# A decoder kernel: in the last cross attention, the scores of both row tiles of a head pair are issued back to back

## The chip, the cores and the metric

The kernel runs on one core of one Trainium2 chip. The metric is the device time of one execution in microseconds (us). Before the change three executions took 4450.89, 4462.71 and 4469.61 us (median 4462.71). For so small an edit the spread matters: the three lie 0.4% apart.

## The reference, cut to what matters

The kernel computes two decoder layers of self attention, cross attention and experts, each behind a layer norm, for 16 sequences of 256 rows and 256 channels. The change touches only the cross attention of the second layer. It has 16 heads of 64 channels; the keys of a sequence are 256 from one source and 256 from a second, 512 in all, and only the first 256 are masked:

```python
k_new = jnp.concatenate([k, gk], axis=1)            # 512 keys per sequence
q = (queries @ Wq.T + bq).reshape(b_s, nq, H, D_K).transpose(0, 2, 1, 3)
att = jnp.einsum('bhqd,bhdk->bhqk', q, k_new) * scale
att_k = jnp.where(attention_mask, -jnp.inf, att[..., :nk])
att = jnp.concatenate([att_k, att[..., nk:]], axis=-1)
att = jax.nn.softmax(att, axis=-1)
out = jnp.einsum('bhqk,bhkd->bhqd', att, v_new)
out = out.transpose(0, 2, 1, 3).reshape(b_s, nq, H * D_V)
return out @ Wo.T + bo
```

## The kernel before, in words

Keys and values of this attention are made in an earlier stage and read back by DMA. The stage itself is `wide_attention_phase`, which writes out one program for each engine. For each sequence `b` it runs 16 steps `s`. A step is one pair of heads (group `g = s // 2`) and one row tile of 128 rows (`t = s % 2`), so that an even step and the odd one behind it share their heads and keys. In this text the even step and the odd step behind it are called a pair of steps, and (8, 9) is the pair of steps 8 and 9.

Each item `n` (one step's work) goes through the engines like this:

- TensorE forms its scores (`scores`, L784): six matmuls of 512 columns into one of two score buffers `s_ps[s % 2]`. A head has 64 channels, so the two heads use the two halves of the array's rows at the same time: three products of two matmuls. It first waits until the buffer has been read (`m_ready`).
- VectorE adds the mask and takes the row maximum (`row_max`, L624), which also frees the score buffer.
- ScalarE takes the exponentials and their sums (`exps`, L714).
- VectorE takes the reciprocals (L685), GpSimd multiplies by them (L581, `n_ready`).
- TensorE transposes the result (`turn`, L796, eight transposes of 128 columns), and VectorE (L630) and ScalarE (L722) copy one half each out of PSUM.
- In a later step TensorE multiplies by the values (L851), ScalarE (L737) and VectorE (L663) take the result.

In step `s` TensorE issues the scores of `s + 2`, the transposes of `s - 1`, and then what the table `AT_STEP` names for the step in one of two banks `a_ps`. At odd steps that is a product with the values (O0 to O7). At even steps it is, in turn: nothing (0), the output projection (2 and 4, L805), the transposes of the normalised rows (6, L835), and the queries of the next sequence (8, 10, 12, 14, L841, Q0 to Q3). The banks are handed back by `a_free`: Q1 for instance waits until VectorE has taken Q0's other half (L647).

The order of each engine is the order in which it is written, with semaphores between them. On ScalarE a step is: exponentials of `s + 1`, copy of transposed `s - 1`, rounding of what the step's bank holds, and at even steps rounding of a key group (L745). On VectorE: reciprocal of `s`, maximum of `s + 2`, copy of `s - 1`, then the work on the banks; `add_output` (L679) in step 4. On GpSimd: multiplication of `s`, and at odd steps the rest of a key group (L575). The sequences 1 to 14 run in a hardware loop of two sequences per turn; the others are written out.

Of the kernel before, what the change touches and what calls it, by code (L numbers as in the profile page):

```python
# [34 lines left out]
TT = S // P  # L35
# [339 lines left out]
def wide_attention_phase(nc, c, x_res, ident, ins, kv):  # L375
# [4 lines left out]
    PAIRS, NS = H // 2, H  # L380
# [3 lines left out]
    with ExitStack() as ctx:  # L384
# [83 lines left out]
        def of(use):  # L468
            return -1 if use in (O7, OUT) else 1 if use == Z or use in QUERIES else 0
# [4 lines left out]
        def emptied(b, use):  # L474
            return (b + 1) * 7 + use // 2 + 2

        def exists(b):
            return not isinstance(b, int) or 0 <= b < B
# [18 lines left out]
        def later(b, s, steps):  # L497

            return b + (s + steps) // NS, (s + steps) % NS

        with nc.Block() as block:
# [263 lines left out]

            @block.tensor
            def _(pe):
                def scores(b, s, u):
                    if not exists(b):
                        return  # L770
                    g, t = s // TT, s % TT
                    n = b * NS + s
                    out = s_ps[s % 2]
                    if t == 0:
                        pe.wait_ge(k_split, b * PAIRS + g + 1)
                    if s % 4 == 0:
                        q = (Q0, Q1, Q2, Q3)[g // 2]
                        pe.wait_ge(a_free[q % 2], emptied(b - 1, q))
                    if not (isinstance(n, int) and n < 2):
                        pe.wait_ge(m_ready, n - 1)  # L780
                    for q_piece, k_piece in PIECES:
                        for i in range(2):
                            lane = slice(i * c.dk, (i + 1) * c.dk)
                            e = pe.matmul(out[:, i, :], qT[q_piece][lane, g, t * P:(t + 1) * P], kT[k_piece][lane, g % KR, :], start=q_piece == 1, stop=q_piece + k_piece == 0, skip_group_check=True)  # L784
                    e.then_inc(s_ready, 1)

                def turn(b, s):
                    if not exists(b):
                        return
                    n = b * NS + s  # L790
                    pe.wait_ge(n_ready, n + 1)
                    for i in range(2):
                        if not (isinstance(n, int) and n < 1):
                            pe.wait_ge(t_done[i], n)
                        for k in range(c.kt):
                            e = pe.transpose(t_ps[i][:, k * P:(k + 1) * P], p[:, s % 4, i, k * P:(k + 1) * P], ident[:, :])  # L796
                        e.then_inc(t_ready[i], 1)

                def output_rows(t, u, step):
                    for g in range(PAIRS):  # L800
                        if t == 0 and g == PAIRS - 1:
                            pe.wait_ge(a_free[O7 % 2], emptied(step, O7))
                        slot = g if g else 8 * (1 - u)
                        for y_piece, w_piece in PIECES:
                            e = pe.matmul(a_ps[OUT % 2][:, t * D:(t + 1) * D], yT[y_piece][:, slot, t * P:(t + 1) * P], wo[w_piece][:, g, :],  # L805
                                          start=g == 0 and y_piece == 1, stop=g == PAIRS - 1 and y_piece + w_piece == 0, skip_group_check=True)
                    return e
# [46 lines left out]

                def body(b, u):
                    for s in range(NS):
                        ahead = later(b, s, 2)
                        scores(*ahead, u if s + 2 < NS else 1 - u)
                        turn(*later(b, s, -1))
                        if s in AT_STEP:  # L860
                            use_bank(b, AT_STEP[s], u)
                        if s == 4 and exists(b + of(OUT)):
                            output_rows(1, u, b).then_inc(a_ready[OUT % 2], 1)

                over_sequences(pe, body)

        nc.clear_and_free_semaphores(own_sems)
# [1727 lines left out]
```

## Time and profile before

| | us |
|---|---|
| median of three runs | 4462.71 |
| the profiled execution | 4456.93 |
| its span in the profile | 4455.9 |
| TensorE busy | 3857.2 (87% of the span) |
| score matmuls L784, 1536 of them, busy | 248.6 |
| first and last start of a score matmul | 2773.2 and 3729.7 |
| transposes L796, 2048 of them, busy | 282.8 |

The execution's time and its span differ by 1 us, so the span can be read as the time. The stage of the change lies between about 2773 and 3757 us of the span. The profile shows one execution; a matmul's start is measured and its end is modelled, so spaces between starts are the safe reading. In a timeline, rows of one kind that stand behind each other on an engine are merged into one ("x6"), and an operation's record often ends some 0.1 us after the next has begun.

### The profile page before, as it was taken

What the parts mean: (1) busy time and instruction counts of PE and PEld (TensorE: products, weight loads), DVE (VectorE), ACT (ScalarE), POOL (GpSimd) and SP (SyncE); (2) the same over time, 40 slices, a digit from 0 to 9 for tenths busy, and PEclk for the clock granted to TensorE, in tenths of its full rate; (3) what the DMA queues carried; (4) which work ended last, traced back from release to release, by engine and by line L of the source; (5) the groups of instructions that cost most, each with busy time, mean ns of one, the idle gap of its engine ahead of it and who ended that gap; (6) DMA issues with size and microseconds to landing.
All of it is one profiled execution on the core that took longest, in us unless ns stands there. A gap on an engine that the chain in (4) does not pass through costs nothing. (4 is left out here: it accounts for less than half of the span.)

```text
span 4455.9 us, 100491 instructions
## 1 busy us (share of the span) xinstructions
PE 3857.2 (87%) x32500; PEld 3115.8 (70%) x32500; DVE 2637.6 (59%) x7922; ACT 1974.4 (44%) x4061; POOL 2233.6 (50%) x2350
## 2 busy tenths in 40 slices
PE   6999799965689999878969997999999997499991
PEld 5777577744478888767757775676666775399991
DVE  4775466658954443345546664766666665855553
ACT  2554255533223333212214444766677764155550
POOL 2332322212146666566644542766667674256665
PEclk8999799977899999989979998999999998599996
DMA  1000000000259999878730001333332331256654
GB/s 54 0 0 1 30 10 12 3 25 21 105 190 298 301 298 301 265 238 266 266 112 1 0 0 64 95 91 90 89 92 73 92 89 32 88 211 226 218 191 120
DMA packets 293460, 518.82 MB, mean 116 GB/s; under 512 B 103008, under 2 KB 136161, under 8 KB 282465
## 3 DMA queue, kind: packets, MB, share of 16 engines
q1 hardware_dynamic: 222656, 353.08, 24.0%
q0 software_dynamic: 37440, 102.29, 8.1%
q10 hardware_dynamic: 33120, 60.31, 3.5%
q8 instruction: 142, 2.33, 0.2%
q14 instruction: 102, 0.83, 0.1%
HBM read 375.55 MB, written 139.98 MB: 116 GB/s over the span
## 5 line engine op out<-in xcount | busy, mean ns | idle before, releaser
L2062 POOL DMA_INDIRECT L_ffn_xin<-zs,L_ffn_listed x460 | 498.6, 1084 | 299.8 <-issue 169.5
L581 POOL TENSOR_TENSOR L_xattn_p<-L_xattn_p,L_xattn_rsum 128x1024 f32<-128x1024 f32 x256 | 484.3, 1896 | 287.8 <-DVE L_xattn_rsum L685 287.8
L2425 POOL DMA_INDIRECT L_ffn_back<-ys,L_ffn_slots x320 | 315.0, 984 | 194.6 <-issue 91.3
L624 DVE CUSTOM_DVE_ANT_0 L_xattn_p<-L_xattn_scores,L_xattn_mask 128x512 f32<-128x512 f32 x512 | 331.6, 685 | 97.8 <-PE L_xattn_scores L784 92.1
L2094 PE MATMUL L_ffn_bank<-L_ffn_xT,L_ffn_w 128*128 128x256 f32 x1528 | 365.9, 383 | 4.8 <-ACT L_ffn_xT L2161 2.9
L714 ACT ACTIVATE L_xattn_p<-L_xattn_p,L_xattn_negmax 128x512 f32<-128x512 f32 x512 | 363.2, 714 | 4.4 <-DVE L_xattn_negmax L624 4.0
L1318 ACT ACTIVATE L_attn_pT<-L_attn_bank 128x384 f32<-128x384 f32 x512 | 223.4, 488 | 295.3 <-PE L_attn_bank L1424 156.3
L2161 ACT ACTIVATE L_ffn_xT<-L_ffn_bank 128x512 f32<-128x512 f32 (+1 forms) x230 | 136.7, 594 | 410.9 <-DVE L_ffn_yo L2323 201.6
L796 PEld LDWEIGHTS L_xattn_turned<-ident,L_xattn_p 128*128 128x128 f32 x2048 | 221.8, 142 | 119.6 <-issue 80.6
L2094 PEld LDWEIGHTS L_ffn_bank<-L_ffn_xT,L_ffn_w 128*128 128x128 f32 x1528 | 277.5, 192 | 38.7 <-issue 5.1
L796 PE MATMUL L_xattn_turned<-ident,L_xattn_p 128*128 128x128 f32 x2048 | 282.8, 282 | 24.1 <-POOL L_xattn_p L581 14.1
L2314 DVE TENSOR_TENSOR L_ffn_hid<-L_ffn_sg,L_ffn_bank 128x256 f32<-128x256 f32 x191 | 80.4, 421 | 329.5 <-issue 199.3
L2067 POOL TENSOR_TENSOR L_ffn_w<-L_ffn_w,L_ffn_w 128x2048 fp32r<-128x2048 f32 x39 | 181.4, 4652 | 166.9 <-ACT L_ffn_w L2187 166.9
L1399 PE MATMUL L_attn_bank<-L_attn_kT,L_attn_qT 32*128 32x128 f32 (+1 forms) x2048 | 247.0, 358 | 16.9 <-DVE L_attn_negmax L1209 11.6
L784 PE MATMUL L_xattn_scores<-L_xattn_kT,L_xattn_qT 64*128 64x512 f32 x1536 | 248.6, 429 | 14.8 <-issue 13.1
L1208 DVE CUSTOM_DVE_ANT_0 L_attn_bank<-L_attn_bank,L_attn_tri 128x128 f32<-128x128 f32 x512 | 160.5, 313 | 167.0 <-PE L_attn_bank L1399 147.3
L851 PE MATMUL L_xattn_bank<-L_xattn_pT,L_xattn_v 128*64 128x256 f32 x2048 | 253.5, 390 | 0.7 <-DVE L_xattn_pT L630 0.7
L1403 PE MATMUL L_attn_bank<-L_attn_qT,L_attn_kT 32*128 32x256 f32 (+1 forms) x2048 | 245.4, 356 | 3.6 <-ACT L_attn_pT L1318 2.4
L1209 DVE CUSTOM_DVE_ANT_0 L_attn_bank<-L_attn_bank,L_attn_tri 128x256 f32<-128x256 f32 x512 | 237.5, 464 | 0.3
L1211 DVE TENSOR_REDUCE L_xattn_negmax<-L_xattn_bank 128x2 f32<-128x512 f32 x256 | 164.6, 685 | 85.6 <-PE L_xattn_bank L1399 84.2
L1318 ACT ACTIVATE L_xattn_pT<-L_xattn_bank 128x512 f32<-128x512 f32 x256 | 139.1, 596 | 143.9 <-PE L_xattn_bank L1421 142.3
L722 ACT ACTIVATE L_xattn_pT<-L_xattn_turned 128x512 f32<-128x512 f32 x256 | 152.3, 595 | 108.3 <-PE L_xattn_turned L796 94.2
(384 smaller groups left out, 11176.5 us busy)
## 6 DMA issues: line engine op xcount, KB each, us to landing
L_ffn_w<-in_L_ffn_w SPq DMA_DIRECT2D x78, 1024.0 KB
L_ffn_w<-in_L_ffn_w SPq DMA_DIRECT2D x191, 384.0 KB
ys<-L_ffn_yo ACTq DMA_DIRECT2D x230, 256.0 KB
kv<-kv_v_row SPq DMA_DIRECT2D x128, 256.0 KB
L_xattn_k_raw<-kv SPq DMA_DIRECT2D x128, 256.0 KB, 2.7
L_xattn_v<-kv SPq DMA_DIRECT2D x16, 2048.0 KB, 9.6
kv<-kv_k_row SPq DMA_DIRECT2D x96, 256.0 KB
L_xattn_mask<-in_L_xattn_mask SPq DMA_DIRECT2D x256, 64.0 KB, 2.0
```

The source lines that it names most:

```text
L581: pool.tensor_tensor(p[:, s % 4, :, :], p[:, s % 4, :, :], rsum[:, s % 2, :, None].to_broadcast([P, 2, c.keys]), ALU.mult).then_inc(n_read ...
L624: e = dve.tensor_tensor_reduce(p[:, s % 4, i, :], s_ps[s % 2][:, i, :], mask[:, s % 4, i, :], SHRINK, 3e38, ALU.add, ALU.min, negmax[:, s ...
L714: e = act.activation(p[:, s % 4, i, :], p[:, s % 4, i, :], ACT.Exp, scale=-1.0, bias=negmax[:, s % 2, i:i + 1], accum_out=lsum[:, s % 2, i ...
L784: e = pe.matmul(out[:, i, :], qT[q_piece][lane, g, t * P:(t + 1) * P], kT[k_piece][lane, g % KR, :], start=q_piece == 1, stop=q_piece + k_ ...
L796: e = pe.transpose(t_ps[i][:, k * P:(k + 1) * P], p[:, s % 4, i, k * P:(k + 1) * P], ident[:, :])
L851: e = pe.matmul(to[i * c.dk:(i + 1) * c.dk, 0:S], values[:, k_, 2 * g + i, :], pT[:, g % 2, i, k_, :], start=k_ == 0, stop=k_ == c.kt - 1, ...
L1318: act.activation(pT[:, h, 0:WIDTH], t_ps[SLOT[2 * g + i]][:, 0:WIDTH], ACT.Exp, scale=c.scale).then_inc(t_taken, 1)
L1399: return pe.matmul(s_ps[SLOT[h]][:, to:to + keys], tile(h, qT[1 - u], t), kT[1 - u][lane(h), h // 4, 0:keys], start=t == 0, stop=t == 1, s ...
L1403: return pe.matmul(t_ps[SLOT[2 * g + i]][:, k * S:k * S + S - q0], tile(h, kT[u], k), qT[u][lane(h), h // 4, q0:S], start=k == 0, stop=Fal ...
L2062: pool.indirect_dma_start(xin[j % U][:, t, :], None, zs, bass.IndirectOffsetOnAxis(ap=listed[:, 2 * j + t:2 * j + t + 1], axis=0)).then_in ...
L2094: return pe.matmul(out, a[0], b[0], start=first, stop=last)
L2425: pool.indirect_dma_start(back[:, i % NG, :], None, ys[0:NB * RB, :], bass.IndirectOffsetOnAxis(ap=slots[:, tile, k:k + 1], axis=0)).then_ ...
```

## The change

`scores` loses an argument that it did not use. Instead of one set of scores per step, TensorE issues at each even step `s` those of `s + 2` and of `s + 3`, and none at the odd steps. All other instructions and all other engines keep their order, and the semaphores and their values are the same.

```diff
-                def scores(b, s, u):
+                def scores(b, s):
...
                 def body(b, u):
                     for s in range(NS):
-                        ahead = later(b, s, 2)
-                        scores(*ahead, u if s + 2 < NS else 1 - u)
+                        if s % TT == 0:
+                            for steps in range(2, 2 + TT):
+                                scores(*later(b, s, steps))
                         turn(*later(b, s, -1))
                         if s in AT_STEP:
                             use_bank(b, AT_STEP[s], u)
```

TensorE's rows for the pair (10, 11) of a sequence before the change (L784 scores, L796 transposes, L841 queries, L851 product with the values, in which two heads merge to x8; REGISTER_ALU computes a value to be waited for):

```order
L784 MATMUL L_xattn_scores<-L_xattn_kT,L_xattn_qT 128x512 x6
L796 MATMUL L_xattn_turned<-ident,L_xattn_p 128x128 x8
L831 REGISTER_ALU
L841 MATMUL L_xattn_bank<-L_xattn_zT,L_xattn_wq 128x256 x12
L780 REGISTER_ALU
L784 MATMUL L_xattn_scores<-L_xattn_kT,L_xattn_qT 128x512 x6
L796 MATMUL L_xattn_turned<-ident,L_xattn_p 128x128 x8
L851 MATMUL L_xattn_bank<-L_xattn_pT,L_xattn_v 64x256 x8
```

And of the changed kernel, the same pair:

```order
L784 MATMUL L_xattn_scores<-L_xattn_kT,L_xattn_qT 128x512 x6
L780 REGISTER_ALU
L784 MATMUL L_xattn_scores<-L_xattn_kT,L_xattn_qT 128x512 x6
L796 MATMUL L_xattn_turned<-ident,L_xattn_p 128x128 x8
L831 REGISTER_ALU
L841 MATMUL L_xattn_bank<-L_xattn_zT,L_xattn_wq 128x256 x12
L796 MATMUL L_xattn_turned<-ident,L_xattn_p 128x128 x8
L851 MATMUL L_xattn_bank<-L_xattn_pT,L_xattn_v 64x256 x8
```

The second score block has moved ahead of the first transposes and of the queries; behind the queries now stand transposes at once. The first transposes and the queries come one score block later than before, the second transposes stand behind the same work as before.

At the pair (4, 5), with the second half of the output projection (L805), TensorE's rows of the changed kernel are:

```order
L784 MATMUL L_xattn_scores<-L_xattn_kT,L_xattn_qT 128x512 x6
L780 REGISTER_ALU
L784 MATMUL L_xattn_scores<-L_xattn_kT,L_xattn_qT 128x512 x6
L796 MATMUL L_xattn_turned<-ident,L_xattn_p 128x128 x8
L805 MATMUL L_xattn_bank<-L_xattn_wo,L_xattn_yT 128x256 x24
L796 MATMUL L_xattn_turned<-ident,L_xattn_p 128x128 x8
L851 MATMUL L_xattn_bank<-L_xattn_pT,L_xattn_v 64x256 x8
```

Here too the second score block stood behind the projection before, and stands ahead of it now, so that the projection ends one score block later after the start of its pair.

## Rows read from the trace of the kernel before

**Rows 1.** The page: busy time and instructions of each engine.

```profile
PE 3857.2 (87%) x32500; PEld 3115.8 (70%) x32500; DVE 2637.6 (59%) x7922; ACT 1974.4 (44%) x4061; POOL 2233.6 (50%) x2350
```

**Rows 2.** One sequence by pairs of steps: (0,1), (4,5) to (10,11), all eight.

```profile
core 0: us, PE busy (x) PEld busy (x) DVE busy (x) ACT busy (x) POOL busy (x), PEclk, DMA share, GB/s
3136.64:3143.47 6.83, 5.78 (x46) 3.75 (x45) 4.97 (x15) 5.03 (x12) 4.85 (x3) 1.00 0.23 66
...
3152.04:3160.62 8.58, 8.58 (x70) 6.63 (x69) 5.73 (x16) 4.91 (x12) 4.55 (x3) 1.00 0.25 72
3160.62:3166.77 6.15, 6.15 (x50) 4.18 (x49) 4.39 (x13) 5.29 (x13) 5.52 (x5) 1.00 0.25 67
3166.77:3173.93 7.16, 7.16 (x58) 5.21 (x57) 4.89 (x14) 5.63 (x14) 6.21 (x4) 1.00 0.19 56
3173.93:3181.22 7.29, 7.29 (x58) 5.22 (x57) 5.08 (x15) 5.63 (x14) 5.02 (x3) 1.00 0.21 54
...
sum 59.16, PE 58.11 PEld 42.06 DVE 40.49 ACT 42.68 POOL 42.22; mean PE 7.26 PEld 5.26 DVE 5.06 ACT 5.34 POOL 5.28
```

**Rows 3.** TensorE's timeline over a pair with queries: start, us, engine, line, operation, tiles.

```profile
3118.25 0.97 PE L784 MATMUL L_xattn_scores<-L_xattn_kT,L_xattn_qT 64*128 64x512 f32 x6
3119.15 1.09 PE L796 MATMUL L_xattn_turned<-ident,L_xattn_p 128*128 128x128 f32 x8
3120.17 1.95 PE L851 MATMUL L_xattn_bank<-L_xattn_pT,L_xattn_v 128*64 128x256 f32 x16
3122.05 0.96 PE L784 MATMUL L_xattn_scores<-L_xattn_kT,L_xattn_qT 64*128 64x512 f32 x6
3122.94 1.09 PE L796 MATMUL L_xattn_turned<-ident,L_xattn_p 128*128 128x128 f32 x8
3123.94 1.69 PE L841 MATMUL L_xattn_bank<-L_xattn_zT,L_xattn_wq 128*128 128x256 f32 x12
```

**Rows 4.** TensorE's timeline, a cut just behind a score block: its first transpose alone.

```profile
3119.15 0.33 PE L796 MATMUL L_xattn_turned<-ident,L_xattn_p 128*128 128x128 f32 x1
```

**Rows 5.** TensorE's timeline, the stage's start: two score blocks behind each other.

```profile
2776.81 1.66 PE L784 MATMUL L_xattn_scores<-L_xattn_kT,L_xattn_qT 64*128 64x512 f32 x12
```

**Rows 6.** TensorE's timeline in the last expert stage: full-array matmuls, then transposes.

```profile
3903.66 0.28 PE L2097 MATMUL L_ffn_bank<-L_ffn_xT,L_ffn_w 128*128 128x256 f32 x1
3903.78 0.60 PE L2088 MATMUL L_ffn_bank<-ident,L_ffn_xin 128*128 128x128 f32 x4
```

**Rows 7.** TensorE's timeline, pair (0,1): the transposes of item 0 and their wait.

```profile
3140.57 1.09 PE L796 MATMUL L_xattn_turned<-ident,L_xattn_p 128*128 128x128 f32 x8 [1.05 <-POOL L_xattn_p L581]
```

**Rows 8.** ScalarE's timeline around the pair of rows 3.

```profile
3122.17 0.39 ACT L737 ACTIVATE L_xattn_yT<-L_xattn_bank 128x256 fp32r<-128x256 f32 x1 [0.56 <-PE L_xattn_bank L851]
...
3125.66 0.84 ACT L734 ACTIVATE L_xattn_qT<-L_xattn_bank,L_xattn_bqs 128x256 fp32r<-128x256 f32 x2 [0.98 <-PE L_xattn_bank L841]
...
3128.32 0.59 ACT L722 ACTIVATE L_xattn_pT<-L_xattn_turned 128x512 f32<-128x512 f32 x1
```

**Rows 9.** VectorE's and GpSimd's timeline in the same pair.

```profile
3123.02 0.86 DVE L647 SCALAR_TENSOR_TENSOR L_xattn_qT<-L_xattn_bank,L_xattn_bqs,L_xattn_qT 128x256 fp32r<-128x256 f32 x2
...
3124.03 3.78 POOL L581 TENSOR_TENSOR L_xattn_p<-L_xattn_p,L_xattn_rsum 128x1024 f32<-128x1024 f32 x2 [2.28 <-DVE L_xattn_rsum L685]
...
3126.72 0.69 DVE L624 CUSTOM_DVE_ANT_0 L_xattn_p<-L_xattn_scores,L_xattn_mask 128x512 f32<-128x512 f32 x1 [0.88 <-PE L_xattn_scores L784]
```

**Rows 10.** VectorE's and GpSimd's timeline, pairs (4,5) and (6,7).

```profile
3157.13 0.69 DVE L679 TENSOR_TENSOR x_res<-L_xattn_bank,x_res 128x512 f32 x1 [1.35 <-PE L_xattn_bank L805]
...
3159.82 1.28 POOL L575 TENSOR_TENSOR L_xattn_kT<-L_xattn_k_raw,L_xattn_kT 128x512 fp32r<-128x512 f32 x1
3161.73 1.90 POOL L581 TENSOR_TENSOR L_xattn_p<-L_xattn_p,L_xattn_rsum 128x1024 f32<-128x1024 f32 x1 [0.62 <-DVE L_xattn_rsum L685]
```

**Rows 11.** TensorE at a turn of the loop, and the clock behind it.

```profile
3198.19 0.96 PE L784 MATMUL L_xattn_scores<-L_xattn_kT,L_xattn_qT 64*128 64x512 f32 x6 [2.31 <-issue]
...
3203.70:3207.10 3.40, 3.40 (x18) 1.85 (x17) 1.01 (x3) 0.68 (x2) 2.40 (x2) 0.50 0.13 30
```

## The prediction

> **What bounds the kernel now.** I read the page first: TensorE is busy for 87% of the span, more than any other engine [rows 1]. The edit touches one stage, so I then cut one of its sequences into its eight pairs of steps. Those stretches sum to 59.16 us with TensorE busy for 58.11, at full clock, while the others work for 40 to 43 [rows 2]. The reader is to see two things there. In seven of the eight pairs TensorE has no idle time at all; and in the pair (0, 1) it has 1.05 us of it, waiting for GpSimd's product of item 0 [rows 2, 7]. So the stage is bound by TensorE's stream, spaces between blocks included, and once per sequence by the chain through softmax.
>
> Busy is not the same as useful, so I read the starts of the blocks. A score block ahead of transposes takes 0.90 and 0.89 us from start to start (3118.25 to 3119.15, 3122.05 to 3122.94) [rows 3]. Where two score blocks stand next to each other, at the stage's start, both together are recorded with 1.66 us against 0.96 or 0.97 for one: the first of two costs 0.70 [rows 3, 5]. The other 0.19 is paid when the array goes from another kind of work to the two half-height matmuls and back.
>
> **The change part by part.** No instruction is added or removed; 128 of the 256 score blocks move ahead of transposes and of an even step's block. The register operation between the two score blocks runs on the sequencer; in rows it stands between blocks that follow each other without a pause, so I cost it at nothing.
>
> *TensorE's own saving in a pair.* The first score block costs 0.70 instead of 0.89: 0.19. Behind the queries (or the projection) came a score block; queries take 7.29 - 3.80 - 1.89 = 1.60 to 1.61 us from start to start (3.80 from the second score block to the next pair's first, 1.89 for scores and transposes ahead of the queries). Their record is 1.69 long, and one such matmul's is 0.28, so the last starts at 1.41 and the score block 0.20 to 0.21 behind it [rows 2, 3, 6]. Now transposes follow, and in the expert stage these start 0.12 behind the last full-array matmul [rows 6]: 0.09 saved. The first transpose behind a score block is recorded with 0.33 us, the four behind full-array matmuls with 0.60 together, as three spaces of 0.11 and one record of 0.27 would be [rows 4, 6]: another 0.05. Sum 0.33 a pair. Neither neighbour occurs in this stage in the form that the change makes, so the bounds: from 0 (the space merely moves) to 0.42 (the next paragraph's 0.09 too). I take 0.33, since both rows are of the same kinds of instruction.
>
> *A wait that goes.* In pairs (10, 11), (12, 13) and (14, 15) the queries start at 3123.94, just when VectorE's work on the bank before ends (3123.02 + 0.86 = 3123.88) [rows 3, 9]. The pair (8, 9), whose bank comes free earlier, is 0.13 shorter [rows 2]. Now the queries come a score block later and I take 0.09 of this as gone.
>
> So for TensorE alone a pair with queries would be: scores at 0 and 0.70, transposes at 1.60, queries at 2.50 (0.90 later), transposes at 4.02 (1.61 - 0.09), values at 4.99 (1.02 - 0.05), end at 6.87 (1.88 for the values [rows 3]), against 7.29.
>
> *What is late next: ScalarE.* The queries end later in the pair, and ScalarE has a row of work behind them. From the start of the queries to L734 it is 1.72 us; from L734 it works through keys and exponentials to the copy L722, 2.66 later, and about 0.5 later it is free for L737 [rows 3, 8]. That is 2.50 + 1.72 + 2.66 + 0.50 = 7.38, where TensorE's values would let L737 start at 6.87 + 0.12 = 6.99. It is 0.39 late. Who waits: from L737 to GpSimd's product it is 1.86 (3122.17 to 3124.03), the product takes 1.90, and transposes follow 0.05 later: 3.81 [rows 8, 9]. Pair (0, 1) bears this out: 0.12 + 3.81 = 3.93 is where its transposes start (3136.64 to 3140.57) [rows 2, 7]. So in the next pair the second transposes cannot start before 0.12 + 0.39 + 3.81 = 4.32, where TensorE would be ready at 4.02. That pair is 7.17 long. In it ScalarE is free at 7.38 again, now only 0.09 behind 7.29, and the pair behind it is short again. Gains against 7.16 and three times 7.29: 0.29, 0.12, 0.42, 0.12.
>
> *Pair (0, 1):* the chain sets it, so TensorE's savings are lost, and it starts 0.09 late: -0.09. *Pair (2, 3):* no rounding behind the projection and no chain near: 0.33.
>
> *Pairs (4, 5) and (6, 7):* the projection now has two score blocks ahead of it, so `add_output`, which started 5.09 into its pair (3152.04 to 3157.13), starts at 5.09 + 0.70 = 5.79, and VectorE's next reciprocal stands behind it [rows 2, 10]. GpSimd's key work starts 2.69 after `add_output` and takes 1.28 [rows 10]; only then comes the product of item 6 (before, it had 0.62 us to spare). So 5.79 + 2.69 + 1.28 + 1.90 = 11.66 for the transposes of item 6, and 2.90 to the pair's end: 14.56, against 8.58 + 6.15 = 14.73 [rows 2]. Gain 0.17, not 0.66. The values of step 5 also wait for `add_output`, inside this bound.
>
> *What loses its cover elsewhere.* The second scores need their buffer at 0.70, read by VectorE in the pair before; its maximum of that item starts 4.67 into a pair, and waits 0.88 for the scores even so [rows 9]. Now those scores come 2.8 us earlier, so that the wait goes and the buffer is free some 2 us ahead. The masks' and keys' DMAs hang on the same maxima and come no later. The first transposes of a pair come 0.7 later and ScalarE's copy of them with them, into the 0.98 us that it was idle ahead of L734 [rows 8]. Cost: nothing in all three.
>
> [...]
>
> *Sum.* -0.09 + 0.33 + 0.17 + 0.29 + 0.12 + 0.42 + 0.12 = 1.36 us a sequence. Fifteen such: 20.4. The last sequence forms no queries and waits for softmax in its later pairs: 0.5. At the stage's start the second scores stand ahead of the last queries, which frees the chain by about one block of queries, 1.6. Together 22.5. From the profiled execution 4456.9 - 22.5 = 4434.4. That execution is 5.8 below the median of the runs; the mean of all four is 4460, which gives 4437.5. I say 4437.
>
> **The rivals.**
> 1. *TensorE alone decides.* For it: it is busy in seven of eight pairs, and the ScalarE chain above is a sum of five durations that may each be shorter without contention. Then 7 x 0.33 + 3 x 0.09 = 2.58 a sequence, 41 with the edges: 4419. The Trainium skill's "TensorEngine Tiling (Array Packing)", section "Key Properties", says that changing the tiling mode drains the engine; by that alone each removed change pays in full, which is this rival. Against it: rows 7 and 8.
> 2. *The spaces only move.* If a second score block costs 0.89 as ever and transposes behind queries start after 0.21, only the wait of 0.09 goes, and ScalarE's lateness takes part of that: 2 to 5 us, 4456. For it: no pair of neighbours in this stage's steady part shows the saving. Against it: rows 5 and 6.
> 3. *Slower, by the clock.* TensorE's idle time in the pair (0, 1) grows from 1.05 to about 1.5 us, since the work stands ahead of it. At turns of the loop, behind an idle time of 2.31 us, the granted clock stood at 0.50 for a stretch of 3.4 us, which is 1.2 GHz [rows 11]. Such a stretch of dense work costs half its length, 1.7 us. It would decide from two in each sequence: 16 x 2 x 1.7 = 54, less 22: 4492. Against it: the clock is 1.00 through an idle time of 1.05 [rows 2, 7].
> 4. *It does not do what it says.* The order shows it does; I leave it 1%.
>
> **How the numbers follow.** Forecast 60%, with its own range 4428 to 4446 (half to one and a half of each chain-bound term, and 4 us for the runs); rival 1 14%, rival 2 20%, rival 3 5%, rival 4 1%. A measurement of this kernel can tell about 0.5%, 22 us, from no change, and the forecast's gain is just that, so its 60% is halved, a little more to faster. Faster: 0.33 + 0.14 = 0.47; same: 0.27 + 0.20 + 0.01 = 0.48; slower 0.05. The range reaches from just under rival 1 to just over rival 2, with the spread of the runs: 4416 to 4461.
>
> **What would show each step.** In the changed profile, two score blocks in a row take 1.66 together, and queries to transposes is 1.52 from start to start. Pairs with queries alternate near 6.87 and 7.17; if all are 6.9, ScalarE was not late; if they are 7.2 and more, the spaces moved. L737 starts more than 0.12 behind the end of the values in every second pair, and TensorE's transposes get a wait for L581 there and in pair (6, 7). Pair (0, 1) stays at 6.8 to 6.9. VectorE's waits for scores go nearly to nothing, without the time following them. What would make me wrong: a wait for `m_ready` between the two score blocks, or a clock below 1.00 in pair (0, 1) away from the loop's turns.

## The result and the profile after

Four executions of the changed kernel took 4425.10 to 4437.77 us, median 4429.81; four of the kernel before 4450.89 to 4469.61, median 4458.64. The ratio is 0.9937, with a 95% interval of 0.992 to 0.9953. In a second measurement, on chip 7, it was 0.9956 (0.9941 to 0.9971). So the change is worth 0.4 to 0.6%, 22 to 29 us. The prediction was 4437 us with a range of 4416 to 4461. The profiled execution took 4437.77 us, the slowest of the four, against 4456.93 for that of before.

In a page's row of an operation stand, behind the bar, its busy time, the mean of one in ns, and the engine's idle time ahead of it with what ended most of that. Of the kernel before:

```profile
L624 DVE CUSTOM_DVE_ANT_0 L_xattn_p<-L_xattn_scores,L_xattn_mask 128x512 f32<-128x512 f32 x512 | 331.6, 685 | 97.8 <-PE L_xattn_scores L784 92.1
L796 PE MATMUL L_xattn_turned<-ident,L_xattn_p 128*128 128x128 f32 x2048 | 282.8, 282 | 24.1 <-POOL L_xattn_p L581 14.1
```

In the changed kernel VectorE's wait for the scores is nearly gone (92.1 to 4.1 us) and the score matmuls' busy time is down from 248.6 us, while TensorE's idle time ahead of the transposes is up from 24.1 us:

```profile
L624 DVE CUSTOM_DVE_ANT_0 L_xattn_p<-L_xattn_scores,L_xattn_mask 128x512 f32<-128x512 f32 x512 | 329.6, 681 | 9.6 <-PE L_xattn_scores L784 4.1
L796 PE MATMUL L_xattn_turned<-ident,L_xattn_p 128*128 128x128 f32 x2048 | 282.2, 282 | 35.6 <-POOL L_xattn_p L581 20.2
L784 PE MATMUL L_xattn_scores<-L_xattn_kT,L_xattn_qT 64*128 64x512 f32 x1536 | 214.9, 412 | 14.1 <-issue 11.8
```

One sequence by its pairs of steps, from (0,1) to (14,15), answers to [rows 2]:

```profile
2833.91:2840.70 6.78, 5.58 (x46) 3.81 (x45) 4.97 (x15) 4.95 (x13) 5.01 (x4) 1.00 0.22 58
2840.70:2848.91 8.21, 8.21 (x70) 6.69 (x69) 5.37 (x17) 4.92 (x12) 5.93 (x6) 1.00 0.76 251
2848.91:2857.39 8.48, 8.29 (x70) 6.89 (x69) 5.63 (x16) 4.91 (x12) 3.88 (x4) 1.00 0.29 92
2857.39:2863.47 6.08, 5.99 (x50) 4.26 (x49) 4.29 (x13) 5.16 (x13) 6.08 (x5) 1.00 0.32 77
2863.47:2870.25 6.78, 6.78 (x58) 5.25 (x57) 4.79 (x14) 5.15 (x14) 6.37 (x5) 1.00 0.23 61
2870.25:2877.46 7.21, 7.00 (x58) 5.26 (x57) 4.97 (x15) 5.96 (x17) 4.93 (x4) 1.00 0.24 57
2877.46:2884.30 6.83, 6.83 (x58) 5.32 (x57) 4.97 (x15) 5.19 (x15) 5.01 (x4) 1.00 0.22 58
2884.30:2891.46 7.17, 6.99 (x58) 5.28 (x57) 4.97 (x15) 5.87 (x16) 5.01 (x4) 1.00 0.22 58
sum 57.55, PE 55.67 PEld 42.74 DVE 39.96 ACT 42.10 POOL 42.22; mean PE 6.96 PEld 5.34 DVE 4.99 ACT 5.26 POOL 5.28
```

The sequence is 1.61 us shorter than the 59.16 of before. The pairs with queries alternate: 6.78, 7.21, 6.83, 7.17. TensorE now has idle time in five of the eight pairs, 1.88 us in all, where it had 1.05 in one. From the first score matmul to the end of the last product with values the stage is 19.5 us shorter in this profile (969.9 to 950.4), and 22.8 to 23.6 shorter in three more profiles of the changed kernel, against the same profile of before. The first of them lost more to the lower clock at the turns of the loop, as the last experiment shows.

TensorE, ScalarE and GpSimd in the pair (8, 9) and the next, in the changed kernel, answer to [rows 3, 8 and 9]:

```profile
2921.04 1.67 PE L784 MATMUL L_xattn_scores<-L_xattn_kT,L_xattn_qT 64*128 64x512 f32 x12
2922.64 1.09 PE L796 MATMUL L_xattn_turned<-ident,L_xattn_p 128*128 128x128 f32 x8
2923.49 1.66 PE L841 MATMUL L_xattn_bank<-L_xattn_zT,L_xattn_wq 128*128 128x256 f32 x12
2924.99 1.04 PE L796 MATMUL L_xattn_turned<-ident,L_xattn_p 128*128 128x128 f32 x8
2925.19 0.84 ACT L734 ACTIVATE L_xattn_qT<-L_xattn_bank,L_xattn_bqs 128x256 fp32r<-128x256 f32 x2 [0.82 <-PE L_xattn_bank L841]
...
2925.96 1.95 PE L851 MATMUL L_xattn_bank<-L_xattn_pT,L_xattn_v 128*64 128x256 f32 x16
2927.84 1.66 PE L784 MATMUL L_xattn_scores<-L_xattn_kT,L_xattn_qT 64*128 64x512 f32 x12
2927.86 0.58 ACT L722 ACTIVATE L_xattn_pT<-L_xattn_turned 128x512 f32<-128x512 f32 x1
2928.34 0.38 ACT L737 ACTIVATE L_xattn_yT<-L_xattn_bank 128x256 fp32r<-128x256 f32 x1
...
2930.20 3.78 POOL L581 TENSOR_TENSOR L_xattn_p<-L_xattn_p,L_xattn_rsum 128x1024 f32<-128x1024 f32 x2 [2.29 <-DVE L_xattn_rsum L685]
...
2932.15 1.09 PE L796 MATMUL L_xattn_turned<-ident,L_xattn_p 128*128 128x128 f32 x8 [0.21 <-POOL L_xattn_p L581]
```

Two things are to be seen. The two score blocks take 1.60 us together to the transposes, and queries to transposes is 1.50: TensorE alone would need 6.78 to 6.83. And L737 starts 0.50 behind the end of the values (2927.84), right behind the copy L722 and with no wait of its own; it started 0.12 behind it before [rows 8]. The product follows 1.86 later, and the transposes stand 4.31 into the new pair, against the 4.32 worked out.

### The profile page after: what moved, and what is told of

Same layout as the page of the kernel before. It is cut to its first block and busy times, and to the rows that moved or that the text cites. A ratio compares the mean times of both kernels' runs of the same rounds, so it can differ in the third digit from the quotient of the medians.

```text
span 4436.1 us, 100491 instructions
## 1 busy us (share of the span) xinstructions
PE 3828.3 (86%) x32500; PEld 3129.7 (71%) x32500; DVE 2627.8 (59%) x7922; ACT 1964.1 (44%) x4061; POOL 2233.2 (50%) x2350
## 3 DMA queue, kind: packets, MB, share of 16 engines
q1 hardware_dynamic: 222656, 353.08, 24.1%
## 5 line engine op out<-in xcount | busy, mean ns | idle before, releaser
L796 PE MATMUL L_xattn_turned<-ident,L_xattn_p 128*128 128x128 f32 x2048 | 282.2, 282 | 35.6 <-POOL L_xattn_p L581 20.2
L796 PEld LDWEIGHTS L_xattn_turned<-ident,L_xattn_p 128*128 128x128 f32 x2048 | 225.4, 142 | 98.0 <-POOL L_xattn_p L581 50.2
L851 PE MATMUL L_xattn_bank<-L_xattn_pT,L_xattn_v 128*64 128x256 f32 x2048 | 256.1, 393 | 3.6 <-DVE x_res L679 2.8
L784 PE MATMUL L_xattn_scores<-L_xattn_kT,L_xattn_qT 64*128 64x512 f32 x1536 | 214.9, 412 | 14.1 <-issue 11.8
L722 ACT ACTIVATE L_xattn_pT<-L_xattn_turned 128x512 f32<-128x512 f32 x256 | 152.1, 594 | 149.1 <-PE L_xattn_turned L796 149.0
```

The costliest lines, as they stand in the source:

```text
L851: e = pe.matmul(to[i * c.dk:(i + 1) * c.dk, 0:S], values[:, k_, 2 * g + i, :], pT[:, g % 2, i, k_, :], start=k_ == 0, stop=k_ == c.kt - 1, ...
```

## The experiments

All were timed in turn with the kernel before, four kernels to a chip: the changed kernel and the next three on chip 7, the four behind those on chip 9, and the single executions at the end on chip 7. The chips differ (the kernel before took 4460.6 us on the first and 4475.6 on the second), so across them only the ratios compare. The yardstick:

> The changed kernel once more, as the yardstick for the runs beside it. Theory A (score blocks that stand side by side save the array's changeover) and theory B (it is enough that the second scores come early) both expect 0.9937 of the kernel before, about 4430 us, and pairs of steps of 6.85, 8.19, 8.45, 6.08, 6.78, 7.21, 6.83 and 7.17 us as in its profile.

Measured: 0.9956 (0.9941 to 0.9971), 4438.9 against 4460.6 us. The pairs' medians were again 6.84, 8.21, 8.45, 6.08, 6.78, 7.21, 6.83 and 7.15.

**Is it the neighbourhood, or that the scores come early?**

```diff
                         if s % TT == 0:
-                            for steps in range(2, 2 + TT):
-                                scores(*later(b, s, steps))
+                            scores(*later(b, s, 2))
                         turn(*later(b, s, -1))
+                        if s % TT == 0:
+                            scores(*later(b, s, 3))
```

> Both score blocks stay in the even step, but the first transposes stand between them: scores, transposes, scores, bank work, then transposes, values. Theory A: the array changes over as often as before the change, so pair (2,3) is 8.5 to 8.6 us (before 8.57, after 8.19), pairs with queries keep only the 0.09 that they no longer wait for their bank, and the time is 4451 to 4460. Theory B: the second scores come almost as early as in the changed kernel, so it keeps its gain: 4430, pair (2,3) 8.2.

Measured: 1.0011 (1.0000 to 1.0022), 4465.0 us. Here are its pairs (2,3), (4,5), (10,11) and (0,1):

```profile
3019.71:3028.28 8.57, 8.57 (x70) 6.61 (x69) 5.37 (x17) 4.91 (x12) 6.04 (x6) 1.00 0.75 263
2968.70:2977.59 8.88, 8.69 (x70) 6.84 (x69) 5.63 (x16) 4.91 (x12) 3.77 (x3) 1.00 0.21 62
2990.93:2998.14 7.21, 7.21 (x58) 5.21 (x57) 4.97 (x15) 5.44 (x17) 4.92 (x4) 1.00 0.21 56
3012.52:3019.71 7.18, 5.78 (x46) 3.75 (x45) 4.97 (x15) 5.38 (x15) 5.01 (x4) 1.00 0.22 55
```

Pair (2,3) is back at the 8.57 of before. So where TensorE alone sets a pair, the whole saving comes from score blocks that stand side by side; scores that merely come early give nothing. The pairs with queries keep the 0.08 to 0.11 by which they no longer wait for their bank (7.18 to 7.21 instead of 7.29). Elsewhere the early scores even cost: (4,5) is 0.30 and (0,1) 0.35 over before. The bank work is even later here than in the changed kernel: the queries start 2.81 into their pair, against 2.45 there and 1.89 before, and ScalarE's L737 starts 0.50 behind the values of the pair ahead. In the changed kernel it did so behind every second pair with queries, here behind each of them, the one ahead of (0,1) too. The pair (10,11):

```profile
2990.93 0.96 PE L784 MATMUL L_xattn_scores<-L_xattn_kT,L_xattn_qT 64*128 64x512 f32 x6
2991.43 0.38 ACT L737 ACTIVATE L_xattn_yT<-L_xattn_bank 128x256 fp32r<-128x256 f32 x1
...
2993.74 1.69 PE L841 MATMUL L_xattn_bank<-L_xattn_zT,L_xattn_wq 128*128 128x256 f32 x12
```

That the work moved back would cost so much I had not expected in this run; it is why it ended just above the range of theory A.

**Does ScalarE's lateness make every second pair wait?** Two moves from the two ends of that chain, each on the changed kernel. On ScalarE, keys ahead of the bank's rounding:

```diff
-                        if s in AT_STEP and AT_STEP[s] != OUT:
-                            round_out(b, AT_STEP[s], u)
                         if s % TT == 0:
                             round_keys(*next_group(b, s))
+                        if s in AT_STEP and AT_STEP[s] != OUT:
+                            round_out(b, AT_STEP[s], u)
```

> The changed kernel, with ScalarE's rounding of a key group ahead of the rounding of the bank in even steps, so that it runs while ScalarE waits for the queries. Theory C (ScalarE is late for the values, and by the chain through VectorE and GpSimd every second pair with queries waits): ScalarE's row behind the queries is 0.52 us shorter, so pairs (10,11) and (14,15) fall from 7.21 and 7.17 to 6.85, pair (0,1) stays at 6.8: 0.7 us a sequence, 11 us, 4419. Theory D (GpSimd's own row of products and keys sets these pairs): they stay at 7.2, 4430.

On VectorE, the queries' bank ahead of the values' bank:

```diff
+                        if AT_STEP.get(s - 1) in QUERIES:
+                            rest_of_queries(b, AT_STEP[s - 1])
                         if use in PAIR_OF:
                             rest_of_values(b, use, u)
...
-                        if AT_STEP.get(s - 1) in QUERIES:
-                            rest_of_queries(b, AT_STEP[s - 1])
```

> The changed kernel, with VectorE's work on the queries' bank ahead of its work on the values' bank in odd steps, which takes 0.78 us out of the chain from the values' end to the next product on GpSimd. Theory C: the pairs with queries no longer wait (all 6.8 to 6.85) though ScalarE is as late as before, and pair (0,1) falls from 6.85 to 6.1 to 6.55: 1.0 to 1.4 us a sequence, 16 to 22 us, 4408 to 4414. Theory D: GpSimd's row is unchanged, pairs (10,11) and (14,15) stay at 7.2, and the time at 4430.

Measured: keys first 0.9917 (0.9901 to 0.9933), 4423.4 us; queries first 0.9899 (0.9883 to 0.9915), 4413.6 us, beside the 4438.9 of the changed kernel. Pairs (10,11) and (0,1), first with keys first, then with queries first:

```profile
2992.71:2999.54 6.83, 6.83 (x58) 5.27 (x57) 4.97 (x15) 5.68 (x15) 4.88 (x4) 1.00 0.24 60
...
3013.20:3020.03 6.83, 5.58 (x46) 3.81 (x45) 4.97 (x15) 4.84 (x13) 5.00 (x4) 1.00 0.23 58
```

```profile
2981.48:2988.28 6.79, 6.79 (x58) 5.26 (x57) 5.06 (x15) 5.53 (x16) 5.06 (x4) 1.00 0.22 60
...
3001.83:3008.17 6.34, 5.58 (x46) 3.81 (x45) 4.20 (x13) 5.29 (x15) 4.92 (x4) 1.00 0.20 62
```

Both remove TensorE's idle time in the pairs with queries, and GpSimd's row, which neither touches, did not set them: theory D falls. Only the VectorE move shortens pair (0,1), as it takes time out of the chain itself. With it the product comes 0.99 behind L737 instead of 1.86:

```profile
2988.77 0.38 ACT L737 ACTIVATE L_xattn_yT<-L_xattn_bank 128x256 fp32r<-128x256 f32 x1
2989.19 0.42 DVE L663 TENSOR_TENSOR L_xattn_yT<-L_xattn_bank,L_xattn_yT 128x256 fp32r<-128x256 f32 x1 [1.64 <-ACT L_xattn_yT L737]
...
2989.76 3.78 POOL L581 TENSOR_TENSOR L_xattn_p<-L_xattn_p,L_xattn_rsum 128x1024 f32<-128x1024 f32 x2 [1.41 <-DVE L_xattn_rsum L685]
```

**The same VectorE move on the kernel before** (the diff above, on the old order):

> The kernel before, with the one change of the run before on VectorE: its work on the queries' bank ahead of its work on the values' bank. The step 'pair (0,1) is set by the chain, the others by TensorE' expects here: pair (0,1) from 6.83 to 6.05 to 6.1, the three pairs whose queries wait for their bank from 7.29 to 7.16 to 7.2, all others unchanged: 1.05 to 1.15 us a sequence, 17 to 18 us, 4442. The rival, that the chain binds only once TensorE's blocks have been moved, expects 4456 to 4460.

Measured: 0.9944 (0.9931 to 0.9957), 4451.5 against 4475.6 us. Pairs (8,9), (10,11), (14,15) and (0,1) of this kernel:

```profile
2997.31:3004.47 7.17, 7.17 (x58) 5.22 (x57) 5.60 (x16) 5.64 (x14) 6.19 (x4) 1.00 0.23 55
3004.47:3011.60 7.13, 7.13 (x58) 5.20 (x57) 5.18 (x16) 5.63 (x14) 5.03 (x3) 1.00 0.19 58
3018.73:3025.86 7.13, 7.13 (x58) 5.19 (x57) 5.18 (x16) 5.64 (x14) 5.02 (x3) 1.00 0.24 59
3025.86:3031.94 6.08, 5.75 (x46) 3.74 (x45) 4.41 (x14) 4.79 (x12) 4.76 (x3) 1.00 0.31 74
```

Pair (0,1) is 0.75 shorter and the queries no longer wait for their bank. So the kernel before lost 0.16 a pair to that wait, not the 0.09 that I took, and this move alone is worth about as much as the whole change; the two intervals overlap. The rival, that the chain binds only once TensorE's blocks have been moved, falls.

**Both moves on the changed kernel:**

> The changed kernel with both moves, keys first on ScalarE and queries first on VectorE. If the chain's terms add up as in the prediction, pair (0,1) is 0.12 + 3.81 - 0.78 + 2.90 = 6.05 (6.34 with the VectorE move alone, where ScalarE was still late), pairs with queries 6.78, the rest as in the changed kernel: 4.6 us under the VectorE move alone, 4409. Rival: the two moves repair the same wait, so that the second adds nothing: 4413.

Measured: 0.9887 (0.9873 to 0.9902), 4427.6 us where before took 4475.6. Pair (0,1) was 6.09 and those with queries 6.77 to 6.78. The interval overlaps with that of queries first alone, so that in time the second move isn't shown; in the profile it is, by 0.25 in pair (0,1). This is the lowest ratio here, though not shown to be lower than that of queries first.

**GpSimd's key work at step 5** (on top of both moves, keys of step 5 behind the product of item 6):

```diff
-                        if s % TT:
+                        if s % TT and s != 5:
                             rest_of_keys(*next_group(b, s - 1))
+                        if s == 6:
+                            rest_of_keys(*next_group(b, 4))
```

> As the run before, and GpSimd does the key group of step 5 after the product of step 6. The prediction's chain for pairs (4,5) and (6,7) (key work of step 5 ahead of product 6) expects that the transposes of item 6 wait 0.1 to 0.2 less, pair (6,7) 5.9 to 6.0 instead of 6.08: 1.5 to 3 us, 4407. If TensorE or another engine sets that pair, 6.08 stays.

Measured: 0.9896 (0.9880 to 0.9912), 4432.5 us: no gain. Pairs (6,7) and (8,9), and then what stands ahead of the transposes of item 6 (lines of the code are two higher here: L632 is the copy, L798 the transposes):

```profile
2990.89:2996.97 6.08, 5.99 (x50) 4.29 (x49) 4.29 (x13) 5.15 (x13) 5.00 (x5) 1.00 0.16 29
2996.97:3004.26 7.29, 7.00 (x58) 5.26 (x57) 5.66 (x16) 5.75 (x15) 7.29 (x5) 1.00 0.36 95
```

```profile
2991.99 1.89 POOL L581 TENSOR_TENSOR L_xattn_p<-L_xattn_p,L_xattn_rsum 128x1024 f32<-128x1024 f32 x1 [1.08 <-DVE L_xattn_rsum L687]
...
2993.26 0.69 DVE L632 COPY L_xattn_pT<-L_xattn_turned 128x512 f32<-128x512 f32 x1
...
2994.09 0.30 PE L798 MATMUL L_xattn_turned<-ident,L_xattn_p 128*128 128x128 f32 x1
```

The product of item 6 now ends at 2993.88, and still the transposes start at 2994.09, 3.20 into the pair as before this move: they follow the end of VectorE's copy of item 5 (2993.95), which the first four of the eight transposes wait for. With both moves alone the product ended 3.13 into this pair and the copy 3.06, and the transposes started at 3.21 too. Two things came late together, and I had seen one. The work moved on GpSimd then fell into pair (8, 9), where GpSimd has no pause at all (7.29 of 7.29) and costs 0.51.

**The order in pair (0,1), and the clock:**

```diff
-                        if s % TT == 0:
+                        if s % TT == 0 and s:
                             for steps in range(2, 2 + TT):
                                 scores(*later(b, s, steps))
+                        elif s < TT:
+                            scores(*later(b, s, 2))
```

> The changed kernel, but with the pair (0,1) in its old order: scores, transposes, scores, transposes, values. If the chain sets that pair, its median stays 6.83 to 6.85 and the time at that of the changed kernel to 3 us. If the longer idle time of TensorE in this pair (1.5 us instead of 1.05) brings the clock down more often at the turns of the loop, the seven loop-turn pairs are shorter here than in the changed kernel by 1 to 5 us together, and fewer stretches at 1.2 GHz are recorded than its seven to nine.

Measured: 0.9928 (0.9916 to 0.9941), 4442.0 us; the changed kernel was not timed on this chip, so the times can't be compared to 3 us. Pair (0,1) was 6.83 as with the change: away from the turns, what the change does in this pair is worth nothing, as the prediction had it. At the loop's turns this pair takes 7.2 to 7.7 us, or over 9. A turn of the changed kernel and the same turn of this one, with the granted clock ahead of the last two numbers:

```profile
3069.01:3078.36 9.34, 7.19 (x44) 4.52 (x45) 3.96 (x12) 3.25 (x8) 5.01 (x3) 0.82 0.12 34
```

```profile
3083.39:3090.69 7.30, 5.75 (x44) 3.74 (x45) 3.96 (x12) 3.24 (x7) 4.76 (x3) 1.00 0.11 30
```

What makes a turn long is not that a stretch at 1.2 GHz falls on it but where. Here is another turn of the changed kernel, the stretch at 1.2 GHz in it and its second transposes with TensorE's wait ahead of them, and then the same two of the long turn above:

```profile
2951.12:2958.70 7.58, 7.11 (x44) 4.84 (x45) 3.96 (x12) 3.02 (x8) 4.76 (x3) 0.78 0.14 41
...
2951.82:2955.27 3.45, 3.45 (x18) 2.30 (x14) 1.67 (x6) 0.00 (x0) 1.69 (x1) 0.51 0.02 7
2955.83 1.06 PE L796 MATMUL L_xattn_turned<-ident,L_xattn_p 128*128 128x128 f32 x8 [0.47 <-DVE L_xattn_pT L630]
...
3074.71:3078.11 3.40, 3.40 (x18) 1.72 (x16) 0.88 (x3) 0.60 (x1) 2.26 (x2) 0.50 0.10 23
3073.85 1.13 PE L796 MATMUL L_xattn_turned<-ident,L_xattn_p 128*128 128x128 f32 x8 [2.15 <-DVE L_xattn_pT L630]
```

In the first the stretch starts 0.7 us into the pair and slows the scores and the first transposes. Behind them TensorE waits for the chain in any case, now 0.47 us instead of 2.15, and the pair is no longer than turns without such a stretch. In the second it starts 5.7 us into the pair and falls on the product with the values, which takes 3.44 us instead of 1.88 with no wait behind it. At all turns over 9 us, of these two kernels and of the one before, this product took 2.8 to 3.6 us, and at all others 1.88.

In the first profiles 5 of 6 such turns were over 9 us with the change and none here, so both kernels were profiled twice more:

> One more look at the changed kernel, to count how often the clock falls in pair (0,1) at the six turns of the loop. If the longer idle time there brings it down more often than the old order of that pair does, four or more of the six pairs are over 9 us, as in its first profile (5 of 6 over 9); if it is chance, the counts of this kernel and of the one with the old order in pair (0,1) overlap.

> One more look at the kernel with the old order in pair (0,1). If the order decides, none or one of the six loop-turn pairs is over 9 us, as in its first profile (0 of 6); if it is chance, up to three as in the kernel before.

> As the first of these looks: four or more of six if the order decides, anything if it is chance.

> As the second of these looks: none or one of six if the order decides, anything if it is chance.

Measured, turns over 9 us: the changed kernel 3 and 3 (and 3 in the yardstick's profile), the old order 3 and 3; the kernel before had 3. The counts overlap, 14 of 24 against 6 of 18, so the order is not shown to matter, and the first pair of profiles can be chance. Times of these four executions were 4456.4 and 4451.5 against 4450.4 and 4446.7, single runs.

The clock has one more place that I had not looked at, the end of the stage. Its last stretch, from the last two rows of scores to the end of the last values, before and with the change:

```profile
3727.17:3743.10 15.93, 12.78 (x103) 8.70 (x101) 7.28 (x20) 8.35 (x20) 7.54 (x4) 1.00 0.01 1
3707.13:3724.68 17.55, 14.21 (x103) 9.86 (x101) 7.25 (x20) 8.13 (x20) 7.54 (x4) 0.90 0.00 1
```

All four profiles of the changed kernel have it at 17.5 to 17.6 us with the clock at 0.90. So do four of the seven other profiles whose score blocks stand side by side; three have 15.9 at 1.00, as have all three without (before, apart, and before with queries first). Whether the change brings this 1.6 us is not shown by so few.

## Why the prediction was right, step by step

- *TensorE's own saving.* Right in kind, and shown by the kernel with the blocks apart. It was put at 0.33 and is 0.35 to 0.39, where nothing else binds: pair (2,3) went from 8.57 to 8.18 or 8.21, and between the two kernels with queries first, in the old and the new order, the pairs with queries go from 7.13 to 6.78. Queries to transposes came to 1.50 instead of 1.52, the transposes behind them to 0.97.
- *The wait that goes.* Mis-sized: 0.09 taken, 0.16 shown by the kernel before with the queries first. Hence the first pair with queries is 6.78, not 6.87.
- *ScalarE late, every second pair waits.* Right in mechanism and size: late by 0.38 (0.39 worked out), the transposes at 4.31 (4.32), pairs alternating, and both ends of the chain moved it as expected. In the second of each two pairs ScalarE was on time, where I had 0.09.
- *Pair (0,1).* No gain, right. The loss of 0.09 did not come (6.83 to 6.85), since ScalarE was on time ahead of it.
- *Pairs (4,5) and (6,7).* The sum was right, 14.56 worked out and 8.45 or 8.48 + 6.08 measured, for a reason that is half of it. The path that I had followed, through GpSimd's key work, is level with one that I had not: `add_output`, the values that wait for it, ScalarE's L737, and VectorE's row up to its copy of item 5. Its start shows as 0.20 us of idle time in (4,5), below; its end is the copy that the transposes of item 6 follow. With GpSimd's key work out of the way nothing changed, so that the sum came out is in part luck.

```profile
2912.24 0.69 DVE L679 TENSOR_TENSOR x_res<-L_xattn_bank,x_res 128x512 f32 x1 [2.05 <-PE L_xattn_bank L805]
...
2913.08 1.95 PE L851 MATMUL L_xattn_bank<-L_xattn_pT,L_xattn_v 128*64 128x256 f32 x16 [0.20 <-DVE x_res L679]
```

- *Cover lost elsewhere.* None, right: VectorE's waits for scores fell from 92.1 to 4.1 us, and TensorE has no wait between the two score blocks (1.66 or 1.67 us for both).
- *The sum.* 1.36 a sequence against 1.61 measured: 4 us over the stage. The two ends of the stage, put at 1.6 and 0.5 us of gain, gave none. Up to the first full sequence the stage took 59.6 to 59.7 us in the four profiles of the changed kernel against 59.8, and the last sequence was 1.0 to 1.1 us longer, with the 1.6 of its last stretch at the lower clock. No run singles out the freed chain at the start that I had counted 1.6 for. The two errors, 4 us one way and 3 the other, nearly cancel: that the stage came out at 22.8 to 23.6 in the profiles with as many long turns as before, where 22.5 was worked out, is luck to that extent. The rest of the distance from 4437 to 4429.8 lies within the spread of the runs, which on chip 7 put the change at 22 us.
- *The rivals.* TensorE alone would have given 4419; the two moves that free the chain show what it was short by. That the spaces only move falls with the 1.60 and 1.50 above. The clock did not make the kernel slower, and away from the turns it stayed at 1.00 in pair (0,1), whose idle time grew from 1.05 us to between 1.20 and 1.27, and not to 1.5. A small cost of the change by the clock is neither shown nor ruled out.

## What to carry to other kernels

Where a busy engine switches between kinds of work, measure start to start across the switch and next to a neighbour of the same kind: here 0.19 us for a score block, and 0.09 and 0.05 behind it. Grouping pays only in the stretches that this engine bounds; the block that is moved back makes others late, and the place to look is whoever follows it in another engine's fixed order. When two arrivals are level, taking one away shows nothing, and the work that was moved needs a place with room.

## What I had not expected of the hardware

The order of two operations on VectorE was worth as much as the change (0.9944 on chip 9 against 0.9956 on chip 7), with 0.75 us a sequence from one pair. And where a stretch at 1.2 GHz falls in a turn of the loop changes from one execution of the same kernel to the next. Early in the pair, ahead of TensorE's wait, it costs nothing that these profiles show; on the product with the values it costs about 1.8 us. That was so at 3 to 5 of 6 turns in four profiles of the changed kernel.
